# Depthwise convolution on TensorE: four 64x64 tiles that skip the empty blocks, output halves exchanged in every second batch, and running maxima in place of accumulators

## Chip, core and metric

The kernel runs on one core of one Trainium2 chip. The metric is the time of one execution in microseconds (us) on that core; the median of three timed runs stands for the kernel. The profile was taken from one more execution. Engines are named as in the profile: PE (TensorE matmul), PEld (TensorE weight load), DVE (VectorE), ACT (ScalarE), POOL (GpSimd), SP (SyncE, which issues the DMAs).

## What is computed

Two blocks in a row on 16 images of 32 channels and 32x32 pixels. The first is a dense block of dilated convolutions, a transform and a 3x3 convolution; the change does not touch it. The second is quantised, and the change is in its middle convolution, the depthwise one:

```python
def _fake_quant(x, bits):
    qmax = 2.0 ** (bits - 1) - 1.0
    scale = jnp.maximum(jnp.max(jnp.abs(x)) / qmax, 1e-08)
    y = x / scale
    yq = jnp.clip(y + jax.lax.stop_gradient(jnp.round(y) - y), -qmax - 1.0, qmax)
    return yq * scale
...
# x (16, 32, 32, 32), w1 (192, 32, 1, 1), w2 (192, 1, 3, 3), w3 (32, 192, 1, 1)
out = jax.nn.relu(_qconv(x, w1))
out = jax.nn.relu(_qconv(out, w2, stride=1, padding=1, groups=PLANES))
out = _qconv(out, w3)
return out + x
```

Each scale is the maximum over a whole tensor, so a convolution can start only when the whole output of the one before it is there and its maximum is known.

## The kernel before

`dense_block` runs first and takes about 346 us of the span. `quantised_block` then runs three stages, c1 (w1), c2 (w2, depthwise) and c3 (w3). The 192 planes are NG = 6 groups of 32, the 16 images are NB = 4 batches of BATCH = 4. The 128 partitions hold 32 channels for each of the four phases q of a pixel (its row and column modulo 2), so that a 3x3 convolution becomes, for each phase of the output, a sum over phases of the input with shifts of 0 or 1.

**c1.** PE multiplies the quantised input `xq` by the weights into PSUM (L1067), ACT (L905) and in every fourth tile DVE (L972) move the result through relu into `I` in SBUF, and DVE keeps a running maximum in `c1_most` (L981). Ahead of c1, DVE rounds the input: L957 and L962 for batches 0 and 1, L962 alone for batches 2 and 3, whose first step is ACT's (L900). At the same time POOL clears `c1_most` (L871), fills `minus_zero` (L872), which releases the semaphore `const`, and builds the first two diagonal weights (`build_diag`, L877).

**c2.** For each group g and batch b, DVE quantises `I` into `q2` (L997, two buffers by g % 2). PE then takes 4 taps t for each half h of the batch, 8 matmuls of 128x128 weights by 512 columns (L1084): partition block (input phase) to partition block (output phase), with a diagonal 32x32 block for each pair. ACT adds the bias, applies relu and writes `I` (L910). DVE reads it back, takes the maximum with an accumulator and writes it again (L1003, `peaks`). POOL builds `diag` for group g + 2 when c2 of group g is done (L877). The 8 PSUM banks hold 4 batches. PE's program for c2 is a loop over pairs of groups; DVE's order is `peaks(g)`, then `quantise(g + 2)`.

**Between c2 and c3.** DVE reduces the 24 maxima (L1016), PE transposes and spreads the result (L1047, L1051), DVE works out the scale (`rescale`), and PE puts the zero point's share into the banks (L1093).

**c3.** DVE and ACT quantise `I` in place (L1036, L916), PE sums over the 6 groups (L1108: 12 matmuls for a batch), DVE scales and adds the residual (L1030), SP stores it.

Order on each engine is the order of the code; engines meet through semaphores. Tile names are shown without numbers in the profile, so `q_c_most` there is `c1_most` (and, in the changed kernel, `c2_most` too).

## Time and profile before

| | us |
|---|---|
| median of 3 runs (lowest to highest) | 451.19 (450.24 to 451.94) |
| the profiled execution | 452.38 |
| its span, first to last instruction | 450.6 |
| PE, DVE, ACT, POOL busy | 395.0, 317.8, 213.6, 65.5 |
| c2, first to last matmul | 47.0 |

The span is what the trace covers; 1.8 us of the profiled execution lie around it. Busy times of the engines overlap each other, so they do not add up to the span: what sets the time in a stage is read from the chain of waits there.

### The profile page before, as it was taken

Reading aid. Unit: us, or ns where it says so; the run is one execution under the profiler, and the core shown is the slowest. Engines: PE = TensorE matmul, PEld = TensorE weight load, DVE = VectorE, ACT = ScalarE, POOL = GpSimd, SP = SyncE. Lnnn points to the kernel's source line nnn. Section 1 sums busy time; section 2 is a strip of 40 time slices with the busy share of each in tenths; the row PEclk is TensorE's granted clock in tenths of the full one; section 3 lists DMA queues with packets and bytes.
Section 4 is the critical chain, followed back from the end, with each engine's and each line's share of the span. In section 5 each row is a group of like instructions: output and inputs, shape, how many; then the busy total and the mean of one; then the engine's idle time right before and its main releaser. Section 6 shows DMA issues by size and latency. Waiting matters only on the chain. (4 is left out here: it accounts for less than half of the span.)

```text
span 450.6 us, 8168 instructions
## 1 busy us (share of the span) xinstructions
PE 395.0 (88%) x2890; PEld 273.3 (61%) x2892; DVE 317.8 (71%) x535; ACT 213.6 (47%) x346; POOL 65.5 (15%) x64
## 2 busy tenths in 40 slices
PE   1977999999999999999999999999494663999966
PEld 1755777687687768768776876877381221344422
DVE  7257666985697398569749857954916998598776
ACT  5135445453734545373454536426254882466550
POOL 6020320302112030211203022000302000001000
PEclk9998999999999999999999999999888697899989
DMA  7355225124432512443250342323000000000004
GB/s 242 87 156 156 66 65 141 52 71 101 127 81 51 156 35 69 102 127 81 61 150 26 75 104 64 83 70 94 1 1 0 1 1 0 0 0 0 0 3 186
DMA packets 19532, 32.54 MB, mean 72 GB/s; under 512 B 4528, under 2 KB 11568, under 8 KB 19504
## 3 DMA queue, kind: packets, MB, share of 16 engines
q1 hardware_dynamic: 19504, 32.17, 27.2%
q8 instruction: 17, 0.28, 0.3%
q14 instruction: 11, 0.09, 0.1%
HBM read 11.38 MB, written 2.10 MB: 30 GB/s over the span
## 5 line engine op out<-in xcount | busy, mean ns | idle before, releaser
L619 PE MATMUL sums_ps<-D,w_hl 128*128 128x512 f32 x576 | 149.5, 415 | 11.8 <-DVE w_hl L542 9.1
L619 PEld LDWEIGHTS sums_ps<-D,w_hl 128*128 128x128 f32 x576 | 109.3, 193 | 52.6 <-issue 14.9
L707 PE MATMUL mix_ps<-mix_hl,F_hl 128*128 128x288 f32 x360 | 66.5, 303 | 6.4 <-DVE St L445 6.0
L300 ACT ACTIVATE r<-sums_ps,bias_sb 64x512 f32<-64x512 f32 x32 | 21.9, 684 | 98.4 <-PE sums_ps L619 96.6
L335 ACT ACTIVATE Y<-mix_ps 128x288 f32<-128x288 f32 x120 | 49.0, 411 | 36.5 <-PE mix_ps L711 24.7
L707 PEld LDWEIGHTS mix_ps<-mix_hl,F_hl 128*128 128x128 f32 x360 | 57.3, 196 | 8.8 <-issue 6.8
L276 POOL CAST X<-X 32x512 fp32r<-32x512 f32 x32 | 27.7, 866 | 149.4 <-ACT X L326 147.8
L1084 PE MATMUL ps<-q_q,q_diag 128*128 128x512 bf16 x192 | 47.0, 408 | 1.5 <-DVE q_q L997 1.5
L401 DVE CAST D<-r 64x512 fp32r<-64x512 f32 x48 | 20.0, 416 | 32.8 <-ACT r L300 32.6
L403 DVE TENSOR_TENSOR D<-r,D 64x512 fp32r<-64x512 f32 x48 | 41.5, 864 | 1.6
L262 POOL TENSOR_TENSOR D<-x_own,D 128x576 fp32r<-128x576 f32 x16 | 25.4, 1607 | 113.9 <-ACT D L343 113.9
L910 ACT ACTIVATE q_I<-ps,w_bias 128x1024 f32 x24 | 26.8, 1115 | 28.3 <-PE ps L1084 28.3
L1084 PEld LDWEIGHTS ps<-q_q,q_diag 128*128 128x128 bf16 x192 | 19.1, 100 | 28.9 <-issue 3.6
L1003 DVE TENSOR_SCALAR_CACHE_REDUCE q_I<-q_I (+1 forms) x24 | 28.9, 1218 | 10.9 <-ACT q_I L910 10.8
L711 PE MATMUL mix_ps<-mix_hl,X 96*128 96x288 f32 x120 | 36.0, 305 | 0.0
L419 DVE SCALAR_TENSOR_TENSOR F_hl<-F,F_hl 128x1024 fp32r<-128x1024 f32 x16 | 19.6, 1224 | 23.1 <-ACT F_hl L317 22.8
L308 ACT ACTIVATE r<-sums_ps,bias_sb 64x512 f32<-64x512 f32 x32 | 22.0, 686 | 27.5 <-PE sums_ps L659 27.4
L428 DVE SCALAR_TENSOR_TENSOR X<-r,X 32x512 fp32r<-32x512 f32 x32 | 32.7, 1021 | 0.7
L659 PE MATMUL sums_ps<-D,w_hl 128*128 128x512 f32 x96 | 30.4, 427 | 2.6 <-DMA D<-D 2.6
L735 PE MATMUL mix_ps<-Y,hc 32*32 32x256 f32 x1080 | 28.8, 381 | 4.1 <-ACT Y L335 4.1
L438 DVE STREAM_TRANSPOSE Zt<-mix_ps 96x1024 f32<-96x1024 f32 x15 | 18.7, 1245 | 18.5 <-PE mix_ps L735 18.5
L735 PEld LDWEIGHTS mix_ps<-Y,hc 32*32 32x32 f32 x1080 | 19.0, 103 | 11.2 <-issue 8.4
(108 smaller groups left out, 445.7 us busy)
## 6 DMA issues: line engine op xcount, KB each, us to landing
D<-D SPq DMA_DIRECT2D x96, 126.0 KB, 2.4
F<-r SPq DMA_DIRECT2D x96, 64.0 KB, 2.0
x_own<-in_x_pads SPq DMA_DIRECT2D x16, 288.0 KB, 4.0
F<-in_x_mix SPq DMA_DIRECT2D x16, 128.0 KB, 2.5
xb<-in_x_res SPq DMA_DIRECT2D x8, 256.0 KB, 2.8
out<-q_res SPq DMA_DIRECT2D x8, 256.0 KB, 2.1
w_raw<-in_w_conv SPq DMA_DIRECT2D x6, 192.0 KB, 4.0
w_raw<-in_w_int SPq DMA_DIRECT2D x1, 843.0 KB, 4.6
```

Source lines behind the costliest of these rows:

```text
L276: nc.gpsimd.tensor_copy(X4[u][64:96, h], X4[u][32 * h:32 * h + 32, h].bitcast(F32)).then_inc(x4_copied[u], 1)
L335: nc.scalar.activation(Y[:, g], banks(p, u)[:, g % 4, 0:MIX], ACT.Copy).then_inc(y_out, 1)
L403: nc.vector.tensor_tensor(out=D[f][u][0:64, 1, :, 2:2 + S], in0=src, in1=D[f][u][0:64, 0, :, 2:2 + S].bitcast(F32), op=ALU.subtract).then_ ...
L428: last = nc.vector.scalar_tensor_tensor(out=X4[u][low, h], in0=r[u][k].rearrange("p a b l -> p (a b l)"), scalar=0.0, in1=X4[u][k, h].bitc ...
L619: last = nc.tensor.matmul(conv_ps[u][:, bank, :], w_hl[:, wp, n, d, :], D[f][u][:, xp, :, 2 * d:2 * d + S], start=start and d == 0 and h == 0,
L659: last = nc.tensor.matmul(bank, w_hl[:, 0, n, d, :], D[f - 1][u][:, 1, :, 2 * d:2 * d + S], start=False, stop=d == 2, skip_group_check=True)
L707: nc.tensor.matmul(y, F_hl[u][:, xp, h, k], mix_hl[:, wp], start=n == 0, stop=False, skip_group_check=True)
L711: nc.tensor.matmul(banks(p, u)[:, g % 4, 0:MIX], X4[u][:, g // 4, NP * (g % 4):NP * (g % 4) + NP], mix4_hl[:], start=False, stop=True, ski ...
L735: last = nc.tensor.matmul(out[32 * dy:32 * dy + 32, j, 0:PX // 4], hc[k, d], Y[k, :, at:at + 32], start=d == 0, stop=d == 2, skip_group_ch ...
L910: nc.scalar.activation(I[:, g, b, 0:PX], ps[:, 2 * b:2 * b + 2].rearrange("p k n -> p (k n)"), ACT.Relu, bias=keep.w2_bias[:, bass.ts(g, 1 ...
L1003: nc.vector.tensor_scalar(I[:, g, b, 0:PX], I[:, g, b, 0:PX], 0.0, 0.0, ALU.max, ALU.max, accum_out=c2_peak[:, g, b:b + 1]).then_inc(c2_pe ...
L1084: last = nc.tensor.matmul(ps[:, 2 * b + h], diag[:, par, 4 * t:4 * t + 4].rearrange("p q c -> p (q c)"), two[:, :, t // 2:t // 2 + PH, t % ...
```

## The change

In c2, two batches are now taken together, in 64x64 tiles. A tile (row, col) reads the partitions 64 * row and up and writes those at 64 * col and up; four such matmuls, one per tile, stand after each other in the code (`quarter`). Of the taps, those whose 64x64 block of weights is all zero are left out: where the input half equals the output phase half (`row == pi`), two taps stay of four. For this to give every tile the same amount of work, the halves of the output are exchanged in every second batch (`pi = col ^ b`). A pair of batches so takes 12 quarters, 48 matmuls of 64x64 by 512 columns, where it took 16 matmuls of 128x128 by 512 columns. Where a tile adds to a bank that the other row of tiles has begun, PE waits for `c2_half` (before quarters 4, 8 and 10). PE's program is written out without a loop; it waits for two batches of `q2` at a time and reports two at a time.

In c3 the odd batches use `w3_swap`, a copy of the weights with exchanged columns, which POOL makes once, behind the first two `build_diag`.

For groups 0 to 4 the maximum is kept in `c2_most` by an elementwise maximum, two tiles in turn; `fold_peaks` reduces it before the last group, whose maxima are taken as before (`last_peaks`). POOL clears `c2_most` (2048 elements a partition) ahead of `minus_zero`.

```diff
@@ -830,7 +830,9 @@
         Iq = I[:].bitcast(BF16)
         c1_peak = sb("c1_peak", [NP, NG // 2 * len(C1_DVE) + 1])
         c1_most = sb("c1_most", [NP, 2, 2, CUT], F16)
-        c2_peak = sb("c2_peak", [NP, NG, NB])
+        c2_peak = sb("c2_peak", [NP, NB + 1])
+        c2_most = sb("c2_most", [NP, 2, PX], F16)
+        w3_swap = sb("w3_swap", [NP, NG, NP], BF16)
         q2 = sb("q2", [NP, 2, NB, SLOT], BF16)
         diag = sb("diag", [NP, 2, 16, C], BF16)
         res = sb("res", [NP, 2, BATCH * PH * PH])
@@ -842,7 +844,8 @@
         stat_ready, turned, top_ready, spread = sem("stat_ready"), sem("turned"), sem("top_ready"), sem("spread")
         f_ready = sem("f_ready")
         x_rounded, x_rounded_dve, xq_ready = sem("x_rounded"), sem("x_rounded_dve"), sem("xq_ready")
-        c1_folded, c2_peaks = sem("c1_folded"), sem("c2_peaks")
+        c1_folded, c2_folded, c2_peaks = sem("c1_folded"), sem("c2_folded"), sem("c2_peaks")
+        c2_half, swapped = sem("c2_half"), sem("swapped")
         c1_done, c1_out, c1_out_dve = sem("c1_done"), sem("c1_out"), sem("c1_out_dve")
         q2_ready, diag_ready = sem("q2_ready"), sem("diag_ready")
         c2_done, c2_out = sem("c2_done"), sem("c2_out")
@@ -869,6 +872,7 @@
         def _(pool):
             nc.gpsimd.memset(zero_pt[:], ZERO)
             nc.gpsimd.memset(c1_most[:], 0.0)
+            nc.gpsimd.memset(c2_most[:], 0.0)
             nc.gpsimd.memset(minus_zero[:], -ZERO).then_inc(const, 1)
 
             def build_diag(g, par):
@@ -880,6 +884,10 @@
 
             build_diag(0, 0)
             build_diag(1, 1)
+            w3 = w_q[:, W1:W3].rearrange("p (g m) -> p g m", m=NP)
+            for half in (0, 64):
+                nc.gpsimd.tensor_copy(w3_swap[:, :, half:half + 64], w3[:, :, 64 - half:NP - half])\
+                    .then_inc(swapped, 1)
             with pool.Fori(0, NG // 2 - 1) as k:
                 for par in range(2):
                     pool.wait_ge(c2_done, k * (2 * NB) + (NB * par + NB))
@@ -920,6 +928,7 @@
         def _(dve):
             dve.sem_inc(c1_out_dve, GRANT)
             dve.sem_inc(c1_folded, GRANT)
+            dve.sem_inc(c2_folded, GRANT)
             done = [0]
 
             def link(ins):
@@ -1000,8 +1009,24 @@
             def peaks(g):
                 for b in range(NB):
                     dve.wait_ge(c2_out, g * NB + (b + 1 + GRANT))
+                    dve.wait_ge(c2_folded, g * NB + (b - 1 + GRANT))
+                    most = c2_most[:, b % 2]
+                    nc.vector.tensor_tensor(out=most, in0=most, in1=I[:, g, b, 0:PX],
+                                            op=ALU.max).then_inc(c2_folded, 1)
+
+            def fold_peaks():
+                dve.wait_ge(c2_folded, (NG - 1) * NB + GRANT)
+                link(nc.vector.tensor_tensor(out=c2_most[:, 0], in0=c2_most[:, 0], in1=c2_most[:, 1], op=ALU.max))
+                half = PX // 2
+                link(nc.vector.tensor_tensor(out=c2_most[:, 1, 0:half], in0=c2_most[:, 0, 0:half],
+                                             in1=c2_most[:, 0, half:PX], op=ALU.max))
+                nc.vector.tensor_reduce(c2_peak[:, NB:NB + 1], c2_most[:, 1, 0:half], AX.X, ALU.max)
+
+            def last_peaks(g):
+                for b in range(NB):
+                    dve.wait_ge(c2_out, g * NB + (b + 1 + GRANT))
                     nc.vector.tensor_scalar(I[:, g, b, 0:PX], I[:, g, b, 0:PX], 0.0, 0.0, ALU.max, ALU.max,
-                                            accum_out=c2_peak[:, g, b:b + 1]).then_inc(c2_peaks, 1)
+                                            accum_out=c2_peak[:, b:b + 1]).then_inc(c2_peaks, 1)
 
             quantise(0, 0)
             quantise(1, 1)
@@ -1011,9 +1036,10 @@
 
                     quantise(k * 2 + (par + 2), par)
             peaks(NG - 2)
-            peaks(NG - 1)
-            dve.wait_ge(c2_peaks, NT)
-            nc.vector.tensor_reduce(stat[:, 2:3], c2_peak[:], AX.XY, ALU.max).then_inc(stat_ready, 1)
+            fold_peaks()
+            last_peaks(NG - 1)
+            dve.wait_ge(c2_peaks, NB)
+            nc.vector.tensor_reduce(stat[:, 2:3], c2_peak[:], AX.X, ALU.max).then_inc(stat_ready, 1)
             rescale(2)
             nc.vector.tensor_tensor(out=last_scale[:], in0=sc[:, 2, 2:3], in1=keep.w_scale[:, 2:3],
                                     op=ALU.mult).then_inc(scale_read, 1)
@@ -1071,22 +1097,33 @@
             spread_stat(1)
             pe.wait_ge(c1_out_dve, NG // 2 * len(C1_DVE) + GRANT)
 
-            with pe.Fori(0, NG // 2) as k:
-                for par in range(2):
-                    pe.wait_ge(diag_ready, k * 2 + (par + 1))
-                    for b in range(NB):
-                        pe.wait_ge(q2_ready, k * (2 * NB) + (par * NB + b + 1))
-                        pe.wait_ge(c2_out, k * (2 * NB) + ((par - 1) * NB + b + 1 + GRANT))
-                        for h in range(2):
-                            two = q2[:, par, b, 2 * h * FIELD:2 * (h + 1) * FIELD]\
-                                .rearrange("p (m l i) -> p m l i", m=2, i=FS)
-                            for t in range(4):
-                                last = nc.tensor.matmul(
-                                    ps[:, 2 * b + h],
-                                    diag[:, par, 4 * t:4 * t + 4].rearrange("p q c -> p (q c)"),
-                                    two[:, :, t // 2:t // 2 + PH, t % 2:t % 2 + PH],
-                                    start=t == 0, stop=t == 3)
-                        last.then_inc(c2_done, 1)
+            def c2_pair(g, two):
+
+                par, sets = g % 2, (g * NB + two) // 2
+                pe.wait_ge(q2_ready, g * NB + two + 2)
+                if g:
+                    pe.wait_ge(c2_out, (g - 1) * NB + two + 2 + GRANT)
+                for n, quarter in enumerate(zip(*(c2_tile(row, col) for row in range(2) for col in range(2)))):
+                    if n in C2_TURNS:
+                        pe.wait_ge(c2_half, sets * 8 + C2_TURNS[n])
+                    for row, col, b, h, pi, u, v, first, final in quarter:
+                        rows = slice(64 * row, 64 * row + 64)
+                        field = q2[rows, par, two + b, 2 * h * FIELD:2 * (h + 1) * FIELD]\
+                            .rearrange("p (m l i) -> p m l i", m=2, i=FS)
+                        at = 4 * (2 * u + v) + 2 * pi
+                        last = nc.tensor.matmul(
+                            ps[64 * col:64 * col + 64, 2 * (two + b) + h],
+                            diag[rows, par, at:at + 2].rearrange("p q c -> p (q c)"),
+                            field[:, :, u:u + PH, v:v + PH], start=first and row == b,
+                            stop=final and row != b, skip_group_check=True)
+                        if final and row == b:
+                            last.then_inc(c2_half, 1)
+                last.then_inc(c2_done, 2)
+
+            for g in range(NG):
+                pe.wait_ge(diag_ready, g + 1)
+                for two in range(0, NB, 2):
+                    c2_pair(g, two)
 
             def zero_points(*banks):
                 for bank in banks:
@@ -1099,13 +1136,15 @@
             zero_points(3, 4, 5)
             pe.wait_ge(scale_read, 1)
             zero_points(6, 7)
+            pe.wait_ge(swapped, 2)
             for b in range(NB):
                 pe.wait_ge(q3_ready, b + 1)
                 pe.wait_ge(q3_act, b + 1)
                 for h in range(2):
                     bank = ps[:, 2 * b + h]
                     for g in range(NG):
-                        last = nc.tensor.matmul(bank, w_q[:, W1 + NP * g:W1 + NP * g + NP],
+                        w3 = w3_swap[:, g] if b % 2 else w_q[:, W1 + NP * g:W1 + NP * g + NP]
+                        last = nc.tensor.matmul(bank, w3,
                                                 Iq[:, g, b, HALF * h:HALF * h + HALF], start=False,
                                                 stop=g == NG - 1, skip_group_check=True)
                     last.then_inc(c3_done, 1)
@@ -1113,6 +1152,20 @@
 
 
 
+def c2_tile(row, col):
+
+
+
+
+
+    for b, h in ((0, 0), (0, 1), (1, 0), (1, 1)) if row == 0 else ((1, 0), (1, 1), (0, 0), (0, 1)):
+        pi = col ^ b
+        taps = [(u, v) for u in range(2) for v in ((row,) if row == pi else (0, 1))]
+        for n, (u, v) in enumerate(taps):
+            yield row, col, b, h, pi, u, v, n == 0, n == len(taps) - 1
+
+
+C2_TURNS = {4: 2, 8: 6, 10: 8}
 C1_TILES = 12
 C1_DVE = [2, 6, 10]
 C1_ACT = [j for j in range(C1_TILES) if j not in C1_DVE]
```

How the instructions stand on the engines, before and after the change. PE in c2, where its program for c2 begins (L1084 is the matmul of before, L1114 that of after):

Before:

```order
L1078 ISA [waits q_diag_ready]
L1084 MATMUL ps<-q_q,q_diag 128x512 [waits q_c2_out,q_q2_ready]
L1084 MATMUL ps<-q_q,q_diag 128x512 x7
L1078 REGISTER_ALU
L1084 MATMUL ps<-q_q,q_diag 128x512 [waits q_c2_out,q_q2_ready]
L1084 MATMUL ps<-q_q,q_diag 128x512 x7
L1078 REGISTER_ALU
```

After:

```order
L1114 MATMUL ps<-q_q,q_diag 64x512 [waits q_q2_ready,q_diag_ready,q_c1_out_dve]
L1114 MATMUL ps<-q_q,q_diag 64x512 x15
L1114 MATMUL ps<-q_q,q_diag 64x512 [waits q_c2_half]
L1114 MATMUL ps<-q_q,q_diag 64x512 x15
L1114 MATMUL ps<-q_q,q_diag 64x512 [waits q_c2_half]
L1114 MATMUL ps<-q_q,q_diag 64x512 x7
L1114 MATMUL ps<-q_q,q_diag 64x512 [waits q_c2_half]
L1114 MATMUL ps<-q_q,q_diag 64x512 x7
L1114 MATMUL ps<-q_q,q_diag 64x512 [waits q_q2_ready]
```

In place of eight matmuls behind each wait there are four stretches of 16, 16, 8 and 8 for a pair of batches, the last three behind `c2_half`, and no register instruction stands between them.

POOL at the start of `quantised_block` (`q_c1_most`, `q_c2_most` and `q_diag` are the tiles above):

Before:

```order
L870 MEMSET q_zero_pt 128x1
L871 MEMSET q_c_most 128x1544
L872 MEMSET q_minus_zero 128x512
L877 TENSOR_TENSOR q_diag<-blocks,w_q 128x512 x2
L883 UNCONDITIONAL_BRANCH
```

After:

```order
L873 MEMSET q_zero_pt 128x1
L874 MEMSET q_c_most 128x1544
L875 MEMSET q_c_most 128x2048
L876 MEMSET q_minus_zero 128x512
L881 TENSOR_TENSOR q_diag<-blocks,w_q 128x512 x2
L889 COPY q_w_swap<-w_q 128x6x64 x2
L891 UNCONDITIONAL_BRANCH
```

A second clearing stands ahead of `q_minus_zero`, whose end releases `const`, and two copies stand behind the two diagonals.

DVE at the end of c2, up to the reduction of the maxima. Before:

```order
L1008 REGISTER_ALU
L1008 COMPARE_AND_BRANCH
L1003 TENSOR_SCALAR q_I,q_c_peak<-q_I 128x1024 [waits q_c2_out] x8
L1016 TENSOR_REDUCE q_stat<-q_c_peak 128x1 [waits q_c2_peaks]
L939 TENSOR_TENSOR q_sc<-q_sc,w_scale 128x1
```

After:

```order
L1014 TENSOR_TENSOR q_c_most<-q_c_most,q_I 128x1024 [waits q_c2_folded,q_c2_out] x4
L1019 TENSOR_TENSOR q_c_most<-q_c_most 128x1024 [waits q_c2_folded]
L1021 TENSOR_TENSOR q_c_most<-q_c_most 128x512 [waits q_chain]
L1023 TENSOR_REDUCE q_c_peak<-q_c_most 128x1 [waits q_chain]
L1028 TENSOR_SCALAR q_I,q_c_peak<-q_I 128x1024 [waits q_c2_out] x4
L1042 TENSOR_REDUCE q_stat<-q_c_peak 128x1 [waits q_c2_peaks]
L948 TENSOR_TENSOR q_sc<-q_sc,w_scale 128x1
```

Three instructions that reduce `c2_most` stand between the maxima of group 4 and those of group 5; the four instructions of group 5 are what they were.

## Rows read from the trace of the kernel before

**Rows 1.** The page: busy us, share of the span, instructions; slices of PE in tenths.

```profile
PE 395.0 (88%) x2890; PEld 273.3 (61%) x2892; DVE 317.8 (71%) x535; ACT 213.6 (47%) x346; POOL 65.5 (15%) x64
...
PE   1977999999999999999999999999494663999966
```

**Rows 2.** The chain of waits in order of time: start us, us, what.

```profile
377.75 0.57 DVE q_c_peak L989
...
381.40 47.01 PE ps L1084 x192
...
428.54 1.12 ACT q_I L910
429.68 1.24 DVE q_I L1003 x2
430.94 0.19 DVE q_stat L1016
```

**Rows 3.** Line L1084 of c2: durations ns min/median/max, first and last start.

```profile
L1084 PEld LDWEIGHTS ps<-q_q,q_diag x192: 95/97/145, 381.4 to 427.8; 128*128 128x128 bf16 x192
L1084 PE MATMUL ps<-q_q,q_diag x192: 390/392/628, 381.4 to 428.0; 128*128 128x512 bf16 x192
```

**Rows 4.** C2 in order of time: start us, us, engine, what, idle before and its releaser.

```profile
380.83 3.54 DVE L997 TENSOR_SCALAR q_q<-q_I,q_sc 128x1158 bf16<-128x1158 f16 x8
...
382.24 0.14 PEld L1084 LDWEIGHTS ps<-q_q,q_diag 128*128 128x128 bf16 x1 [0.28 <-issue]
382.66 0.14 PEld L1084 LDWEIGHTS ps<-q_q,q_diag 128*128 128x128 bf16 x1 [0.28 <-issue]
...
403.28 1.21 DVE L1003 TENSOR_SCALAR_CACHE_REDUCE q_I<-q_I  x1
...
404.41 1.22 DVE L1003 TENSOR_SCALAR_CACHE_REDUCE q_I<-q_I  x1
```

**Rows 5.** Stretches of c2, all and L1084: length, busy (x touching), granted clock, DMA.

```profile
386.00:388.00 2.00, 2.00 (x8) 0.74 (x7) 1.23 (x2) 0.26 (x1) 0.00 (x0) 0.69 0.00 0
...
390.00:424.00 34.00, 34.00 (x149) 14.30 (x148) 1.00 0.00 0
```

**Rows 6.** Tiled matmuls of the transform, in order of time.

```profile
155.37 1.91 PE L735 MATMUL mix_ps<-Y,hc 32*32 32x256 f32 x72 [0.59 <-ACT Y L335]
...
160.33 1.91 PE L745 MATMUL mix_ps<-Zt,hr 96*32 96x256 f32 x16
```

**Rows 7.** Line L735: durations ns min/median/max.

```profile
L735 PE MATMUL mix_ps<-Y,hc x1080: 371/374/399, 64.8 to 334.5; 32*32 32x256 f32 x180
```

**Rows 8.** C1 in order of time, on ACT and on DVE, instructions that follow without a break.

```profile
364.62 6.47 ACT L905 ACTIVATE q_I<-ps 128x772 f32 x9 [0.54 <-PE ps L1067]
...
360.45 1.97 DVE L981 TENSOR_TENSOR q_c_most<-q_c_most,q_I 128x772 f16<-128x772 f16 x4
```

**Rows 9.** Line L1108 of c3 in a stretch: PE busy (x touching), PEld, granted clock, DMA.

```profile
439.00:444.40 5.40, 5.19 (x24) 1.95 (x22) 1.00 0.54 197
```

**Rows 10.** Start of the quantised block in order of time.

```profile
346.21 1.38 POOL L871 MEMSET q_c_most<- 128x1544 f16 x1
...
348.13 2.05 POOL L877 TENSOR_TENSOR q_diag<-blocks,w_q 128x512 bf16<-128x512 bf16 x2
...
349.30 1.50 DVE L957 TENSOR_SCALAR q_x_rnd<-fields,q_sc 128x1158 f32<-128x1158 f32 x1
...
351.51 0.82 DVE L957 TENSOR_SCALAR q_x_rnd<-fields,q_sc 128x1158 f32<-128x1158 f32 x1
```

**Rows 11.** POOL and DVE in the dense block, in order of time.

```profile
142.14 3.23 POOL L262 TENSOR_TENSOR D<-x_own,D 128x576 fp32r<-128x576 f32 x2 [15.89 <-ACT D L343]
142.18 1.92 DVE L403 TENSOR_TENSOR D<-r,D 64x512 fp32r<-64x512 f32 x1
```

**Rows 12.** Line L403: durations ns min/median/max.

```profile
L403 DVE TENSOR_TENSOR D<-r,D x48: 683/684/1924, 14.6 to 307.3; 64x512 fp32r<-64x512 f32 x48
```

**Rows 13.** The stretch after c2: length, busy PE, PEld, DVE, ACT, POOL, granted clock.

```profile
431.60:435.00 3.40, 3.40 (x9) 1.16 (x8) 1.92 (x8) 0.59 (x1) 0.00 (x0) 0.50 0.00 0
```

## The prediction

> **What bounds the kernel now.** I read the page's totals and slices first, then the chain of waits over the last 70 us, then c2 by stretches and in order of time. PE is busy for 88% of the span [rows 1], but the change touches only what comes after the dense block, from 346 us on. In the chain [rows 2], one piece stands out: PE's 192 matmuls of c2, 47.0 us from 381.40, without a break. Behind them come ACT's last batch, DVE's last maximum and the reduction at 430.94, 2.53 us after PE's end (428.41). So c2 is bound by PE, and each microsecond taken from its matmuls moves the end, until ACT or DVE become the bound.
>
> Two paces hold in c2. The granted clock is 0.5 (1.2 GHz) at first; its mean of 0.69 in the stretch from 386 to 388 [rows 5] puts the rise at about 387.2, 5.8 us after the first matmul. Until then matmuls follow each other by 0.427 us (the weight loads at 382.24 and 382.66 [rows 4]; the rows are rounded to 0.01). After it the clock is 1.0 (2.4 GHz) and 149 matmuls touch 34.0 us, the first and last in part [rows 5]: 0.230 us each. Check: 5.8 / 0.427 = 13.6 matmuls at the low clock, the other 178.4 at 0.230 make 41.0, and 0.2 for the end of the last: 47.0, as the chain has it.
>
> ACT and DVE have slack. A batch comes every 8 x 0.230 = 1.84 us; ACT needs 1.12 of it [rows 2]. DVE takes 1.13 for a maximum where two follow each other (403.28, 404.41) and (3.54 - 0.52) / 7 = 0.43 for a quantisation (eight in 3.54, the last one's own 0.52 taken off) [rows 4]: 1.56 of 1.84. DVE is the one that would bind next if it kept its work.
>
> **The change part by part.**
>
> *Matmuls.* A pair of batches takes 12 quarters in place of 16 full matmuls, so c2 takes 144 quarters in place of 192 matmuls. What a quarter costs is the question of this case: four 64x64 matmuls of 512 columns, each with its own weights. The trace of before has no bf16 tile of 64x64. The nearest rows are the transform's 32x32 tiles: 72 matmul records of 256 columns, 12 tiles, pass in 1.91 us [rows 6], though one lasts 0.374 [rows 7]. One after another at 0.230 / 512 = 0.45 ns a column they would take 8.3 us. They did run beside each other, six rounds of twelve in (1.91 - 0.37) / 6 = 0.26 us or less, with a weight load for each, in the same order of code (rows of tiles, then columns) that the change uses. So I take the pace of a quarter to be that of one full matmul with the same columns and the same strides, 0.230. The low end is 0.216, the pace of c3's matmuls, whose columns lie in one piece (24 in 5.19 us of busy time [rows 9]). The high end: a tile waits for its weights, 0.097 us a load [rows 3], so 0.327.
>
> From the first matmul on: 5.8 us at the low clock hold 13.6 quarters, the other 130.4 at 0.230 take 30.0, and 0.2 for the last: 36.0 in place of 47.0, **-11.0**. The first matmul now waits for two quantised batches, one more at 0.43: **+0.4**.
>
> *The waits on `c2_half`.* Quarter 4 may start when quarter 1 has ended. Quarter 1 ends 0.39 after its start, [rows 3]; quarter 4 is due 3 x 0.230 = 0.69 after that start. 0.3 us are left for the semaphore (0.1 from PE's end at 428.41 to ACT's start at 428.54 [rows 2]) and the weight loads (0.1). Quarter 10 waits for quarter 7 in the same way, quarter 8 has longer. The cover is thin: between 0 and 0.1 us each, 24 tight waits, 0 to 2.4 us; I take 0.03 each, **+0.7**. Only PE's own matmuls stand behind these waits.
>
> *ACT.* Its 24 instructions stay, but two become due at once. Back to back it does nine tiles of 772 elements in 6.47 us [rows 8]: (6.47 - 0.85) / 8 = 0.70 each, or 0.93 for 1024. Both banks' worth are out 0.1 + 0.93 + 1.11 = 2.1 us after a pair ends, and PE wants those banks 12 x 0.230 = 2.76 after it. Cost 0; if quarters fell to 0.18, ACT would set the pace.
>
> *DVE.* The elementwise maximum of 772 half-precision elements takes (1.97 - 0.56) / 3 = 0.47 [rows 8], so 0.62 for 1024. A pair costs 2 x (0.62 + 0.43) = 2.1 of 2.76 us: hidden. The quantised group g + 2 is there about 4 us after c2 of g ends, and is wanted after 5.5. With the old maxima it would have been 2 x 1.56 = 3.1 of 2.76, so this edit carries the other.
>
> *The end of c2.* ACT now does the last two batches after PE's last matmul, in place of one: batch 3 is out after 2.1 in place of 1.2. Ahead of the last maxima DVE folds `c2_most`: c1's reduction of 386 elements took 0.57 [rows 2], its maximum of 772 takes 0.56 with its own end [rows 8]; by length 0.70 (1024), some 0.44 (512) and 0.70 (the reduction of 512), 1.9 with their links. Group 4's last batch is out 3.4 before PE's end, folded at -0.7; then four maxima at 1.13 start at -0.7, 0.4, 1.6 and 2.7, and the last needs 1.26 (429.68 to 430.94). That is 3.95 after PE's end where 2.53 was: **+1.4**. If DVE were in time it would be +1.1.
>
> *The start of c1.* POOL now clears 2048 more elements (1.38 x 2048 / 1544 = 1.84 us) before `minus_zero`, and makes two copies behind the diagonals (by the two diagonals, 2.05 for 2 x 512 elements, some 0.7 each). `const` comes at about 350.4, DVE asks for it after 352: no wait. But POOL and DVE get in each other's way. The same rounding takes 1.50 beside POOL's diagonals and 0.82 after them [rows 10]. A DVE instruction whose median is 0.684 [rows 12] once took 1.92 [rows 11] and ended at 144.10, between the ends of two POOL instructions (142.14 to 145.37, so the first near 143.6): they take turns. The Trainium skill says so too (SBUF — State Buffer, "Who interferes with whom"): of a VectorE two-port instruction and a GpSimd one, the second to issue fully blocks. The trace agrees with it.
>
> In turns, DVE's six rounding instructions (0.6 to 0.7 each: 1.50 from 349.30 is 0.62 past the diagonals' end at 350.18) now meet clearing, `minus_zero`, two diagonals and two copies, where they met one diagonal. Counted through in turns, the first `xq` is there at about 351.3, where it was 351.6, and the last some 2.3 us later than before. c1's fifth tile, which needs all four, had 0.7 us of slack on it. ACT then runs nearly without a break [rows 8], so nothing gives this back: **+1.5**, between -0.5 (no meeting at all) and +3 (DVE gets no turn until POOL is through).
>
> *Free.* `w3_swap` is ready some 60 us early; c3 has the same matmuls. POOL's later diagonals take 1.03 [rows 10] against 4 us of slack. PE's code for c2 has no loop any more; parts of the dense block are written out as well, and PE's slices there stand at 9 [rows 1], so I price its fetching at 0.
>
> **Sum:** -11.0 + 0.4 + 0.7 + 1.4 + 1.5 = **-7.0 us**. The profiled execution took 452.38 (span 450.6), so the same one would take 445.4. It lies 1.2 above the median of the runs; 451.19 - 7.0 gives **444.2**.
>
> **The rivals.**
>
> *Weight loads show (slower).* If a tile cannot take new weights while its matmul runs, each quarter grows by up to a load, 0.097: 144 x 0.097 = +14, or +12.7 for the 130 at the high clock. The sum is then about +6: 457. It decides from 0.284 a quarter, since 7.0 / 130.4 = 0.054. For it: no row has 64-column loads, and the 96x32 tiles of rows 6 take 1.91 us for only 16 records, 0.4 for a round of four (their input is strided). Against it: the rounds of twelve.
>
> *PE drains at `c2_half`.* If each of the 36 waits lets the tiles run dry, each costs the end of a matmul (0.39 - 0.23 = 0.16) and a new start (0.1): 36 x 0.26 = 9.4 in place of 0.7, so 452.9. The burst of rows 6, which has both ends, costs 1.91 / 6 = 0.32 a round. Against it: the 0.3 us of cover.
>
> The Trainium skill has a rule that comes out there (TensorE: Matmul & The Clock Gate, "Measured speedup vs the span model"): four row tiles of 512 columns gained 3.07 times, not four. An estimate from that page: 4 x 0.230 / 3.07 = 0.30 a quarter, +9.1 on the sum. The trace does not bear it out where rounds follow each other; a single burst is nearer to it.
>
> *Half of the weight loads shows.* 0.28 a quarter: +6.5, so 450.7, not to be told from before.
>
> *DVE starves at the start of c1.* +1.5 more: 445.7.
>
> *The clock in c3.* Before, it was 0.5 from 431.6 to 435.0 [rows 13], and 1.0 in c3 [rows 9]. PE now idles 1.4 us longer there. If it comes back one such stretch later, the first batch of c3 takes 0.427 in place of 0.216 for 12 matmuls, +2.5, of which DVE hides little: 446.5.
>
> *Cheaper quarters.* At 0.216 and no stall, or no meeting with POOL: -2 to -3: 441.5.
>
> **How the numbers follow.** My forecast 0.53; c3's clock 0.12; DVE starved 0.10; cheaper 0.06; PE drains 0.07; weight loads in full 0.05; half of them 0.07. The last three, 0.19, are left out of the range: 440.5 (below the cheap case) to 449.5 (two of the dear ones together). About 0.5%, 2.3 us, is what a measurement can tell from no change. Below 448.9 lie the first four, 0.81, and a little of the half: faster 0.82. Between lie the rest of the half and a part of the drained case, 0.09; above, weight loads in full and the other part, 0.09.
>
> **What would show it.** c2 from first to last matmul near 36 us (0.327 a quarter gives 48.6, 0.216 gives 34); batches' ACT in pairs every 2.76; DVE idle in c2; PE's end to the reduction 3.6 to 4.0; the first ACT instruction of c1's steady run 1.5 later after the dense block. I am wrong if quarters cost over 0.25, if PE stops at quarters 4 and 10, or if the clock stays at 0.5 with tiles.

## The result, and the profile after

The changed kernel takes 444.6 us (median of 4 runs, 443.8 to 445.4), the kernel before on the same chip 450.7. The ratio on record is 0.985, with a 95% interval from 0.983 to 0.987 (the two medians alone give 0.986), so the kernel is faster by 1.3 to 1.7%. The forecast was 444.2, faster. Its profiled execution took 444.73 us, with a span of 442.9 where [rows 1] had 450.6: 7.7 less.

The page of the changed kernel: busy us of PE, and the slices of PE and of its granted clock in tenths, to be laid beside [rows 1].

```profile
PE 385.4 (87%) x3274; PEld 274.4 (62%) x3276; DVE 310.1 (70%) x518; ACT 212.6 (48%) x346; POOL 71.2 (16%) x67
...
PE   1978999999999999999999999999687285599686
...
PEclk9998999999999999999999999999969589599959
```

The line of c2's matmuls in the changed kernel (durations ns min/median/max), against [rows 3].

```profile
L1114 PEld LDWEIGHTS ps<-q_q,q_diag x576: 102/105/168, 382.0 to 416.6; 64*64 64x64 bf16 x192
L1114 PE MATMUL ps<-q_q,q_diag x576: 387/388/633, 382.1 to 416.8; 64*64 64x512 bf16 x192
```

There are three times as many matmuls and loads, each as long as one of before, so four matmuls must run at once. ACT's rows in c2 of the changed kernel in order of time (start us, us, engine, line, what, idle before and its releaser) give the pace of a pair of batches.

```profile
389.72 2.12 ACT L918 ACTIVATE q_I<-ps,w_bias 128x1024 f32 x2 [0.63 <-PE ps L1114]
...
398.02 2.12 ACT L918 ACTIVATE q_I<-ps,w_bias 128x1024 f32 x2 [0.66 <-PE ps L1114]
...
400.78 2.12 ACT L918 ACTIVATE q_I<-ps,w_bias 128x1024 f32 x2 [0.63 <-PE ps L1114]
```

Four pairs from 389.72 to 400.78 are 2.765 us a pair, 0.2304 for each of twelve quarters. ACT idles for 0.63 in each, so PE still sets the pace.

Stretches of the changed kernel: length, busy us of PE, PEld, DVE, ACT, POOL, granted clock, DMA. They answer to [rows 5, 13].

```profile
384.00:386.00 2.00, 2.00 (x24) 0.94 (x20) 0.51 (x2) 0.00 (x0) 0.00 (x0) 0.50 0.00 0
386.00:388.00 2.00, 2.00 (x40) 1.10 (x36) 0.00 (x0) 1.02 (x2) 0.00 (x0) 1.00 0.00 0
...
420.00:424.00 4.00, 2.30 (x7) 1.09 (x9) 1.93 (x7) 0.00 (x0) 0.00 (x0) 0.52 0.01 2
424.00:428.00 4.00, 3.26 (x9) 0.95 (x8) 3.86 (x7) 3.10 (x3) 0.00 (x0) 0.50 0.00 0
428.00:432.00 4.00, 4.00 (x15) 1.51 (x14) 1.75 (x4) 1.54 (x2) 0.00 (x0) 0.70 0.17 66
```

In c2 the clock rose at 386.0, 3.9 us after the first matmul (5.8 before). Behind c2 it fell to 0.5 and stayed there until about 430, well into c3. The forecast had left the time of that stage unchanged. The chain of waits of the changed kernel (start us, us, what) shows the end of c2 and the first batch of c3, against [rows 2]. The fence behind it has PE's rows of c3's first two batches in order of time.

```profile
412.84 1.12 ACT q_I L918
413.98 0.70 DVE q_c_most L1014
414.71 0.70 DVE q_c_most L1019
415.43 0.44 DVE q_c_most L1021
415.89 0.69 DVE q_c_peak L1023
416.58 4.57 DVE q_I L1028 x8
```

```profile
426.62 4.58 PE L1147 MATMUL ps<-q_I,w_q 128*128 128x512 bf16 x12 [0.74 <-DVE q_I L1062]
...
431.04 2.76 PE L1147 MATMUL ps<-q_I,q_w_swap 128*128 128x512 bf16 x12
```

The four last maxima on DVE now set the end of c2. The first batch's 12 matmuls take 4.58 us, the second's 2.76.

Last, the start of the quantised block in the changed kernel in order of time, against [rows 10].

```profile
346.40 1.81 POOL L875 MEMSET q_c_most<- 128x2048 f16 x1
...
347.90 0.92 DVE L966 TENSOR_SCALAR q_x_rnd<-fields,q_sc 128x1158 f32<-128x1158 f32 x1
...
348.14 1.14 POOL L876 MEMSET q_minus_zero<- 128x512 bf16 x1
...
349.36 2.95 POOL L881 TENSOR_TENSOR q_diag<-blocks,w_q 128x512 bf16<-128x512 bf16 x2
349.82 1.59 DVE L966 TENSOR_SCALAR q_x_rnd<-fields,q_sc 128x1158 f32<-128x1158 f32 x1
...
351.45 3.44 DVE L971 TENSOR_SCALAR q_xq<-q_x_rnd 128x1158 bf16<-128x1158 f32 x3
352.26 2.01 POOL L889 COPY q_w_swap<-w_q 128x384 bf16<-128x384 bf16 x2
```

Both engines are stretched: POOL's two diagonals take 2.95 where [rows 10] has 2.05, one rounding 1.59 where it is 0.82 without a neighbour.

The balance, from the two profiled executions (us). "Block" is DVE's reduction of the first statistic of the quantised block, from which c1 is counted:

| piece | before | after | difference | forecast |
|---|---|---|---|---|
| dense block, up to "block" | 346.5 | 345.5 | -1.0 | 0 |
| block to c2's scale (c1) | 34.23 | 35.42 | +1.2 | +1.5 |
| scale to c2's first matmul | 0.64 | 1.17 | +0.5 | +0.4 |
| c2, first to last matmul | 47.00 | 35.13 | -11.9 | -10.3 (-11.0, waits +0.7) |
| PE's end to the reduction | 2.54 | 3.97 | +1.4 | +1.4 |
| reduction to the last result | 17.14 | 19.27 | +2.1 | 0 |

Before rounding, the differences add up to -7.64, and the span shows -7.65. The first row is scatter: the same code of the dense block reached "block" between 344.5 and 348.2 in the thirteen profiles of this study.

### The profile page after: what moved, and what is told of

The parts are those of the page before. It is cut to its first block and busy times, and to the rows that moved or that the text cites. A ratio compares the mean times of both kernels' runs of the same rounds, so it can differ in the third digit from the quotient of the medians.

```text
span 442.9 us, 8893 instructions
## 1 busy us (share of the span) xinstructions
PE 385.4 (87%) x3274; PEld 274.4 (62%) x3276; DVE 310.1 (70%) x518; ACT 212.6 (48%) x346; POOL 71.2 (16%) x67
## 5 line engine op out<-in xcount | busy, mean ns | idle before, releaser
L403 DVE TENSOR_TENSOR D<-r,D 64x512 fp32r<-64x512 f32 x48 | 41.5, 865 | 1.6
L1114 PE MATMUL ps<-q_q,q_diag 64*64 64x512 bf16 x576 | 35.1, 403 | 2.0 <-DVE q_q L1006 2.0
L918 ACT ACTIVATE q_I<-ps,w_bias 128x1024 f32 x24 | 25.4, 1111 | 19.2 <-PE ps L1114 19.2
L735 PE MATMUL mix_ps<-Y,hc 32*32 32x256 f32 x1080 | 28.8, 381 | 4.1 <-ACT Y L335 4.1
L1114 PEld LDWEIGHTS ps<-q_q,q_diag 64*64 64x64 bf16 x576 | 19.8, 109 | 16.9 <-issue 3.6
L735 PEld LDWEIGHTS mix_ps<-Y,hc 32*32 32x32 f32 x1080 | 19.0, 103 | 11.2 <-issue 8.4
L1093 PE MATMUL ps<-q_xq,w_q 128*128 128x386 bf16 x72 | 17.4, 381 | 9.1 <-DVE q_xq L971 5.2
```

The lines of the kernel that those rows point to most:

```text
L403: nc.vector.tensor_tensor(out=D[f][u][0:64, 1, :, 2:2 + S], in0=src, in1=D[f][u][0:64, 0, :, 2:2 + S].bitcast(F32), op=ALU.subtract).then_ ...
L735: last = nc.tensor.matmul(out[32 * dy:32 * dy + 32, j, 0:PX // 4], hc[k, d], Y[k, :, at:at + 32], start=d == 0, stop=d == 2, skip_group_ch ...
L1093: last = nc.tensor.matmul(c1_slot(ps, j)[:, h], w_q[:, bass.ts(k * 2 + par, NP)], xq[:].rearrange("p b n -> p (b n)")[:, at:at + CUT], sta ...
L1114: last = nc.tensor.matmul(ps[64 * col:64 * col + 64, 2 * (two + b) + h], diag[rows, par, at:at + 2].rearrange("p q c -> p (q c)"), field[: ...
```

## The experiments

"c1", "c2", "end of c2" and "c3" are the pieces of that table. All kernels are made from the changed one. Those that add matmuls for PE overwrite their results; none leaves a part of the computation out.

### Is c2's gain the skipped blocks, and what do the maxima carry?

**All taps.** The tiles and their order stay, but the empty blocks are computed too, 16 quarters a pair.

```diff
-        taps = [(u, v) for u in range(2) for v in ((row,) if row == pi else (0, 1))]
+        taps = [(u, v) for u in range(2) for v in (0, 1)]
-C2_TURNS = {4: 2, 8: 6, 10: 8}
+C2_TURNS = {8: 4, 12: 8}
```

> The changed kernel with no tap left out: each tile does four taps for every half, the empty 64x64 blocks too, so 16 quarters for a pair of batches in place of 12; c2_half is waited for before quarters 8 and 12. Theory (a quarter costs what one full matmul costs, tiles by themselves give nothing): c2 grows by 48 quarters x 0.230 = 11 us, to about 46, and the time to 455.6, above the kernel before by the 5 us that c1's start, the end of c2 and c3's clock cost. Rival (tiles are cheaper in themselves): below 453.

Measured: 456.27 us, 1.0068 of before (1.0032 to 1.0103); c2 took 47.07. ACT in c2 of this kernel in order of time:

```profile
397.01 2.12 ACT L918 ACTIVATE q_I<-ps,w_bias 128x1024 f32 x2 [1.57 <-PE ps L1114]
...
400.69 2.12 ACT L918 ACTIVATE q_I<-ps,w_bias 128x1024 f32 x2 [1.56 <-PE ps L1114]
```

A pair comes every 3.68 us, 16 x 0.230. Four 64x64 matmuls cost what one 128x128 costs, and without the skipping the tiles gain nothing: c2 is as long as before (47.00), and the rest of the change (c1 +1.2, first matmul +0.5, end +1.2, c3 +2.4) makes the kernel slower. The whole gain is the quarter of the work that is left out.

**Tiles with the old maxima.** DVE goes back to the maximum with accumulator, and the fold is gone.

```diff
-                    nc.vector.tensor_tensor(out=most, in0=most, in1=I[:, g, b, 0:PX],
-                                            op=ALU.max).then_inc(c2_folded, 1)
+                    nc.vector.tensor_scalar(I[:, g, b, 0:PX], I[:, g, b, 0:PX], 0.0, 0.0, ALU.max, ALU.max,
+                                            accum_out=c2_peak[:, bass.ts(g * NB + b, 1)])\
+                        .then_inc(c2_peaks, 1)
...
-            fold_peaks()
-            last_peaks(NG - 1)
+            peaks(NG - 1)
```

> The changed kernel with the maxima of before: all 24 by the instruction with an accumulator that also writes its input back, no c2_most kept and none folded (POOL still clears it). Theory (tiles need the cheap maxima): DVE needs 2 x (1.13 + 0.43) = 3.1 us for a pair, PE 2.77, so DVE sets the pace in the middle of c2; c2 gets 3 to 4 us longer, less 0.3 at its end: 447.5 to 448.5. Rival (PE sets the pace anyway): 444.3.

Measured: 448.64 us, 0.9942 (0.9918 to 0.9966); c2 took 38.97. DVE in c2 of this kernel, in order of time:

```profile
400.32 2.61 DVE L1006 TENSOR_SCALAR q_q<-q_I,q_sc 128x1158 bf16 x4
402.85 1.21 DVE L1012 TENSOR_SCALAR_CACHE_REDUCE q_I<-q_I  x1
...
407.41 2.55 DVE L1006 TENSOR_SCALAR q_q<-q_I,q_sc 128x1158 bf16 x4
```

DVE never idles here: a group takes 407.41 - 400.32 = 7.1 us, where PE needs 2 x 2.765 = 5.5. So DVE becomes the bound. It also costs clock. c2 began with 3.4 us at 0.5, a little less than the changed kernel's 3.9. Between 407 and 411 PE then waited for `q2` and was busy for only 1.9 of 4 us, and from 410.3 to 413.7 the granted clock was at 0.5 once more, in the middle of c2. That second stretch can be worth at most 1.7 of the 3.8 us that c2 is longer; how the 3.8 divide between DVE's pace and the clock isn't shown, but both come from DVE.

**The maxima with the old matmuls.** PE's loop of before, everything else of the change.

```diff
-            for g in range(NG):
-                pe.wait_ge(diag_ready, g + 1)
-                for two in range(0, NB, 2):
-                    c2_pair(g, two)
+            with pe.Fori(0, NG // 2) as k:
...
+                            for t in range(4):
+                                last = nc.tensor.matmul(
+                                    ps[:, 2 * b + h],
+                                    diag[:, par, 4 * t:4 * t + 4].rearrange("p q c -> p (q c)"),
```

> The changed kernel with the 128x128 matmuls of before (the loop too) and the old weights in c3; running maxima, folding and POOL's clearing and copies stay. Theory (the matmuls carry the whole gain): c2 47 us as before, c1 1.2 us longer, so about 452, not under 450.7. Rival (the maxima are part of the gain by themselves): under 450.

Measured: 453.54 us, 1.0036 (1.0005 to 1.0066). In its chain of waits c2 is one piece again:

```profile
382.93 46.55 PE ps L1110 x192
```

c2 is bound by PE, as before; the running maxima gain nothing there, and POOL's added work costs its 1.2 us at c1. Neither half of the change brings the whole gain alone: the ratios are 0.994 and 1.004, together 0.985.

### How do the tiles share PE's queue?

The forecast rested on matmuls of different tiles standing next to each other in the code. If the overlap needs that, two matmuls of a tile in a row must break it.

```diff
-                for n, quarter in enumerate(zip(*(c2_tile(row, col) for row in range(2) for col in range(2)))):
+                four = [list(c2_tile(row, col)) for row in range(2) for col in range(2)]
+                for n in range(0, 12, 2):
+                    quarter = [t[m] for t in four for m in (n, n + 1)]
```

> The changed kernel with the same 48 matmuls for a pair in another order: each tile gets two of its matmuls in a row before the next tile's turn. Theory (PE starts matmuls strictly in order, so only neighbours in different tiles overlap): two quarters take four times 0.23 in place of twice, c2 doubles from 35 to about 68 us, and the time is near 476. Rival (each tile takes its own from the queue): 444.6, as the changed kernel.

Measured: 445.31 us, 0.9818 (0.976 to 0.9875); c2 36.02. ACT in c2 of this kernel in order of time:

```profile
395.43 2.12 ACT L918 ACTIVATE q_I<-ps,w_bias 128x1024 f32 x2 [0.65 <-PE ps L1116]
398.18 2.12 ACT L918 ACTIVATE q_I<-ps,w_bias 128x1024 f32 x2 [0.63 <-PE ps L1116]
...
400.96 2.12 ACT L918 ACTIVATE q_I<-ps,w_bias 128x1024 f32 x2 [0.65 <-PE ps L1116]
```

(400.96 - 395.43) / 2 = 2.765, the same pace to three figures. My theory fell and the rival held: the order of the code can't be the order of the starts, or the pace would be twice as long. A tile's next matmul must be passed by the other tiles' ones. c2 is 0.9 longer only because 5.9 us of it, not 3.9, ran at the low clock. How far does that go? Four in a row (`range(0, 12, 4)`, and the waits on `c2_half` set to `{4: 6, 8: 8}`):

> The changed kernel with four matmuls of a tile in a row before the next tile's turn; to keep the banks apart, c2_half is then waited for before the 5th and 9th of each tile, for all that stands before. Two in a row had left the pace at 2.77 us a pair. Theory (each tile takes its own matmuls from a queue that holds them all): 16 matmuls still take 4 x 0.23, and two full waits for the tiles to run dry add about 0.3 us each, so 3.4 us a pair, c2 43 us, the time about 452. Rival (only near neighbours overlap): 16 matmuls take nearer to 2 us or more, a pair 6 us and up, c2 over 70 us, the time over 480.

Measured, one run: 453.18 us. PE in c2 of this kernel in order of time:

```profile
390.97 3.37 PE L1116 MATMUL ps<-q_q,q_diag 64*64 64x512 bf16 x48 [0.20 <-PE ps L1116]
...
394.54 3.37 PE L1116 MATMUL ps<-q_q,q_diag 64*64 64x512 bf16 x48 [0.20 <-PE ps L1116]
```

3.57 us a pair, and 44.4 us for c2: dearer than 2.765, but far from 48 x 0.230 = 11 one after another, and near the theory's 3.4. The same view shows where the 0.80 goes. First one stretch of 16 matmuls between two waits, then the weight loads of PE; each of these rows begins as a wait ends.

```profile
408.83 1.15 PE L1116 MATMUL ps<-q_q,q_diag 64*64 64x512 bf16 x16 [0.20 <-PE ps L1116]
```

```profile
394.54 0.64 PEld L1116 LDWEIGHTS ps<-q_q,q_diag 64*64 64x64 bf16 x16 [0.71 <-PE ps L1116]
...
395.83 1.58 PEld L1116 LDWEIGHTS ps<-q_q,q_diag 64*64 64x64 bf16 x32 [0.65 <-PE ps L1116]
...
398.11 0.64 PEld L1116 LDWEIGHTS ps<-q_q,q_diag 64*64 64x64 bf16 x16 [0.71 <-PE ps L1116]
```

The 16 matmuls between two waits take 1.15: three steps of 0.23 and the last one's own 0.39 make 1.08, so four matmuls of a tile in a row still run at the pace of the changed kernel. From one wait to the next, 394.54 to 395.83, are 1.29 us for four rounds (0.92); the next eight rounds take 2.28 (1.84). So the two waits of a pair cost 0.37 and 0.44, together the whole 0.80: at each the tiles run dry, and PE has no matmul for 0.14 to 0.20 of it. No limit to what can wait at a tile shows up to four.

### What the start of c1 costs

POOL's clearing of `c2_most` goes behind c1's last matmul, and the two copies behind the later diagonals.

```diff
-            nc.gpsimd.memset(c2_most[:], 0.0)
...
+            pool.wait_ge(c1_done, NG // 2 * C1_TILES)
+            nc.gpsimd.memset(c2_most[:], 0.0).then_inc(c2_zeroed, 1)
...
+            dve.wait_ge(c2_zeroed, 1)
```

> The changed kernel with POOL's new work moved: c2_most is cleared once c1's matmuls are done, and w3_swap is copied behind the last diagonal. Nothing else differs. Theory (POOL and DVE block each other at the start of c1): the stretch from the start of the quantised block to the end of c1 was 1.2 us longer than before and loses that again, so about 443.4 where the changed kernel has 444.6; the fifth tile of c1 starts some 1.5 us sooner. Rival (the clock, or nothing in particular, made c1 longer): c1 as long as in the changed kernel, 444.6.

Measured: 444.99 us, 0.985 (0.9817 to 0.9884). The start of the quantised block of this kernel, in order of time:

```profile
349.68 2.04 POOL L880 TENSOR_TENSOR q_diag<-blocks,w_q 128x512 bf16<-128x512 bf16 x2
...
350.84 1.50 DVE L967 TENSOR_SCALAR q_x_rnd<-fields,q_sc 128x1158 f32<-128x1158 f32 x1
...
353.05 0.82 DVE L967 TENSOR_SCALAR q_x_rnd<-fields,q_sc 128x1158 f32<-128x1158 f32 x1
...
353.90 2.11 DVE L972 TENSOR_SCALAR q_xq<-q_x_rnd 128x1158 bf16<-128x1158 f32 x3
```

These are the durations of [rows 10] again; three roundings take 2.11, not 3.44. c1's fifth tile starts 8.53 us after "block" (before 8.63, changed 9.55), and c1 is 34.45 long: 0.97 of the 1.19 are back. So POOL's added work was the main cause. It wasn't the only one, because c1 also begins at the low clock: the clock rose 10.0 us after "block" in the kernel before, 13.2 in the changed one and 11.7 in this one. In the profile of the next kernel, with POOL's work where the change has it (fifth tile at 9.55 again) but the clock back at 10.3, c1 took 34.82; in the eight others with POOL's work there and the clock back at 11.75 to 13.6 it took 35.42 or 35.43. So POOL's work costs 0.6 us where the clock comes back early and 1.0 where it comes back late; the rest of the 1.2 is the clock's. The median doesn't show that microsecond: it is less than the scatter of the runs, and in the profile the dense block ended 2.7 us later.

### What the clock in c3 costs

PE gets 18 matmuls behind c2, so that it is not idle while ACT and DVE finish.

```diff
+            pe.wait_ge(c2_out, NT - 2 + GRANT)
+            for n in range(18):
+                nc.tensor.matmul(ps[:, 0], keep.w3_sum[:], minus_zero[:], start=True, stop=True,
+                                 skip_group_check=True)
```

> The changed kernel with 18 extra matmuls of 128x128 by 512 columns into PSUM bank 0, which is free there, between c2 and the transpose of the maxima, where PE otherwise idles 4.3 us. Their result is overwritten. Theory (the late rise of the clock costs c3's first batch 2.1 us): the granted clock stays at 1.0, the 12 matmuls of the first batch take 2.8 in place of 4.6 us, and the time is about 442.5. Rival (c3's first batch is late for its input, or the reduction of the maxima is what costs): 444.6, or 445 and more if the extra matmuls stand in the way of the transpose.

Measured: 443.32 us, 0.9822 (0.9771 to 0.9873). PE behind c2 of this kernel in order of time (the record of one of the 18 is missing):

```profile
418.75 3.83 PE L1136 MATMUL ps<-q_minus_zero,w_sum 128*128 128x512 bf16 x17 [0.16 <-issue]
...
427.06 2.75 PE L1151 MATMUL ps<-q_I,w_q 128*128 128x512 bf16 x12 [1.35 <-DVE q_I L1062]
```

The first batch takes 2.75 in place of 4.58, and the small matmuls of the scale are quicker too: c3 is 16.50 long, not 19.27. The 2.77 us are shown in the profile. The intervals of the two ratios overlap, but the granted clock of every run agrees: its mean over the span was 0.958 to 0.969 in the four runs here and 0.950 to 0.954 in the ten runs of the changed kernel. Was the slow first batch chance? The changed kernel, run again:

> The changed kernel as it is, beside e11 on the same chip, to see how its time spreads: by its first runs a ratio of 0.985 to the kernel before, 0.983 to 0.987. Theory (c3's first batch at the low clock is the usual case): the profile again has 12 matmuls in 4.3 to 4.9 us there. Rival (it was one draw): 2.8 us.

Measured: 444.38 us, 0.985 (0.9817 to 0.9882). The stretch and PE's row of the first batch in this run:

```profile
424.00:428.00 4.00, 3.26 (x8) 0.90 (x7) 3.14 (x2) 4.00 (x4) 0.00 (x0) 0.50 0.00 0
```

```profile
425.52 4.45 PE L1147 MATMUL ps<-q_I,w_q 128*128 128x512 bf16 x12 [0.74 <-DVE q_I L1062]
```

It is the usual case, though not the only one, as the next kernel shows.

### Can the end of c2 be shorter?

The fold moves ahead of group 4, whose maxima then use the accumulator like group 5's.

```diff
-                dve.wait_ge(c2_folded, (NG - 1) * NB + GRANT)
+                dve.wait_ge(c2_folded, (NG - 2) * NB + GRANT)
...
-            peaks(NG - 2)
             fold_peaks()
+            last_peaks(NG - 2)
             last_peaks(NG - 1)
```

> The changed kernel with the running maxima folded after group 3; groups 4 and 5 both take their maxima with the accumulator. Theory (DVE is late for the last maxima by the folding): from PE's last matmul to the reduction 3.6 in place of 3.97 us, the time about 444.2. Rival (ACT's last batch sets it): 3.97 as it is.

Measured, one run: 443.12 us, the end of c2 4.71 long. DVE there, in order of time:

```profile
412.16 1.21 DVE L1028 TENSOR_SCALAR_CACHE_REDUCE q_I<-q_I 128x1024 f16<-128x1024 f16 x1
...
420.13 1.22 DVE L1028 TENSOR_SCALAR_CACHE_REDUCE q_I<-q_I 128x1024 f16<-128x1024 f16 x1
...
421.39 0.16 DVE L1042 TENSOR_REDUCE q_stat<-q_c_peak 128x1 f32<-128x9 f32 x1
```

The theory fell. Eight maxima at 1.14 now stand in a row, 9.1 us from the end of the fold, and DVE has no slack to hide them in; the changed order, with four, is the better. The run was quick all the same because in it the clock was at 1.0 in c3 (first batch 2.75, c3 17.44) and c2 had 2.9 us at the low clock: an example of how one run misleads.

### Together

First all of it (POOL late, the early fold, 16 matmuls between c1 and c2, 18 ahead of c3):

> The changed kernel with POOL's new work moved as in e1, extra matmuls before c3 as in e2, 16 more of them between c1 and the spreading of its maxima, and the folding after group 3. Theory: -1.2 at the start of c1, -2.1 in c3, -0.3 at the end of c2, and about -2 in c2, whose first 3.9 us ran at the low clock: 444.6 - 5.6 = 439. Rival (the clock falls anyway in the gaps that are left before c2, or the extra matmuls delay what follows): 441 or more.

Measured: 441.93 us, 0.9748 (0.9691 to 0.9806): the rival held. Two stretches of this kernel:

```profile
382.00:386.00 4.00, 3.84 (x40) 2.24 (x44) 2.60 (x7) 0.00 (x0) 0.00 (x0) 0.57 0.00 0
...
428.00:432.00 4.00, 4.00 (x15) 1.61 (x14) 1.89 (x4) 1.42 (x2) 0.00 (x0) 0.74 0.19 70
```

The clock fell in both places although PE had been given work: between that work and c2, and in c3, PE still idled for the scale. c3's first batch took 4.44, with the same 18 matmuls ahead of it that had been enough in the profile above. The end of c2 was 4.91, the early fold's. The last kernel drops the fold, and puts work also into those gaps: 9 matmuls ahead of c1, 16 and 7 around the scale of c2, 18 and 3 around that of c3.

```diff
+            busy(9, w_q[:, 0:HALF])
...
+            busy(16, minus_zero[:])
             spread_stat(1)
+            busy(7, minus_zero[:])
...
+            pe.wait_ge(c2_out, NT - 2 + GRANT)
+            busy(18, minus_zero[:])
...
+            busy(3, minus_zero[:], 6)
```

> The changed kernel with POOL's new work moved as in e1 and PE kept busy in its gaps by matmuls whose results are overwritten: 9 ahead of c1, 16 and 7 around the spreading of c1's maxima, 18 ahead of the transpose of c2's, 3 before the last zero points; the folding stays where the change has it. Theory (what is left of the cost is POOL against DVE at the start of c1, and the clock in c2 and c3): c1 1.0 us shorter, c2 33.5 in place of 35.1, c3 2.8 shorter: 444.6 - 5.4, about 439. Rival (the clock falls all the same, or the matmuls stand in the way): 442 or more.

Measured: **437.66 us** (436.85 to 441.84, 6 runs), 0.9708 of before (0.9667 to 0.9748), on the chip where the changed kernel had 0.985 (0.9817 to 0.9882). Two stretches of this kernel, the first just behind the start of c2 (379.35) and the second around that of c3 (421.18):

```profile
380.00:384.00 4.00, 4.00 (x77) 2.28 (x72) 1.96 (x6) 1.53 (x2) 0.00 (x0) 1.00 0.02 4
...
420.00:424.00 4.00, 3.29 (x17) 1.31 (x15) 3.48 (x4) 4.00 (x4) 0.00 (x0) 1.00 0.00 0
```

c1 is 32.89 long, c2 33.35 (144 x 0.2304 and the last one's own end), c3 16.50: against the profile of the changed kernel -2.5, -1.8 and -2.8, together 7.1, and the profiled executions differ by 444.73 - 437.49 = 7.2. c1 gained 1.5 us more than the forecast had for it: the clock was back 5.5 us after "block", and 1.0 of the 2.5 is POOL's moved work.

## Why the prediction was right, step by step

**The matmuls, -11.0 and +0.7; measured -11.9.** The pace of 0.230 a quarter, the question of the case, was right to the third figure. The row that it leaned on carries less than the prediction made of it. Six rounds of twelve have five steps between them, so [rows 6] give (1.91 - 0.37) / 5 = 0.31 us a round, not 0.26, while 256 columns at 0.45 ns each are 0.115. They show that tiles run beside each other, not that a round costs what one matmul costs; that was a guess until the kernel with all taps showed it (47.07 against 47.00). Two sizes were off. The waits on `c2_half` cost nothing: a pair takes 12 x 0.2304 with three waits in it, so 0.3 us of cover is enough (-0.7). And the low clock lasted 3.9 us, not the 5.8 carried over from before (-0.9); in the other profiles of kernels with tiles, the last one aside, it lasted between 2.9 and 5.9 at the start of c2. Half of that difference is time, so the term scatters by 1.5 us from run to run, which the forecast did not allow for.

**The dear rivals.** Neither weight loads nor draining showed: loads of 0.105 stay hidden under running matmuls, also of the same rows of the array. Where the tiles do run dry, in the kernel with four in a row, a wait costs 0.4, more than the 0.26 of that rival. The Trainium skill says otherwise of loads and order in TensorE: Matmul & The Clock Gate, "What overlaps and what doesn't": weight loads overlap only where the row group differs, and matmuls start and end strictly in order. Here four tiles without a pause have a matmul running on each row group at each load, and the pace is 4.0 matmuls in the time of one; two in a row of one tile keep it, where strict order would have made some 476 us of the kernel. The measurement decides. Nor do these four tiles, in a stream, gain the 3.07 times of four row tiles that the prediction took from the Trainium skill (same page, "Measured speedup vs the span model"): they gain 4.0. No run has a single burst of four, so what one would gain is not shown.

**The start of c2, +0.4; measured +0.5.** As forecast.

**DVE and ACT hidden in c2.** Both held; the tiles with the old maxima show that one edit carries the other. The forecast of 3.1 us a pair for the old maxima was low, since a quantisation of four takes 2.6 beside POOL's diagonal; measured 3.5.

**The end of c2, +1.4; measured +1.4** (3.97, forecast 3.95), by the chain that was named: fold, then four maxima in a row.

**The start of c1, +1.5; measured +1.2.** The first tile came earlier (4.69 after "block", before 5.35) and the fifth later (9.55, before 8.63), as counted in turns. That is 0.9; the other 0.3 is the clock, which rose later and which the forecast for c1 left out.

**c3, 0; measured +2.1. This step failed.** The rival with 0.12, priced at +2.5, is what happened in 7 of the 9 profiles of kernels with the change or a part of it and no work added ahead of c3. The prediction put the term at 0 and gave no reason but that before the clock had come back by 435.0. What the runs show in its place: the clock came back at 430.4, 3.7 us into c3, and the 12 matmuls of the first batch took 4.58 in place of 2.76. Work for PE ahead of c3 took it away in two of the three profiles that had such work (2.75, and 4.44 with all put together). Whether the clock comes back in time isn't settled by the length of the gap alone. From c2's last matmul to c3's first are 7.7 and 8.0 us in the two kernels with the old matmuls, where the batch was quick; 8.2 to 9.4 in the seven profiles where it was slow; but 10.2 in the kernel with the early fold, where it was quick again. What else decides it stays open.

So the total is right partly by luck: +2.1 in c3 stands against -0.7 of waits that were free, -0.9 of a shorter low clock, -0.3 at c1 and -1.0 of scatter in the dense block. With c3's cost added to the forecast it would have been 446.3; the range held both.

## What to carry to other kernels

Zero blocks of 64x64 can be left out at full value: count the blocks, give each of the four tiles the same number (no run here tried unequal ones), and price a round of four as one full matmul. A gain of PE shows in full only if the engine behind it keeps up, here because it was relieved in the same step. Every gap that the change opens in PE's work is to be priced with the clock of the stage behind it; where it falls, matmuls with no use in the gap can be worth nearly as much as the change itself (here 0.985 to 0.971, of which about 1 us was POOL's moved work). A piece of POOL's work that is needed later does not belong beside DVE's work on the path.

## What the runs showed of the hardware

- The four tiles take their matmuls independently of the order of the code: one or two in a row of a tile give 2.765 us for 48. Four in a row give 3.57, all of the difference at the two waits; 16 matmuls between waits still take four steps of 0.23.
- A wait of PE on its own matmuls of three rounds back costs nothing (three of them in 12 x 0.2304); a wait on those just issued costs 0.4.
- The granted clock after a gap is not the same from run to run: with tiles and no work in the gaps c2 began with 2.9 to 5.9 us at 0.5 (1.2 GHz), and c3's first batch took 2.75 or 4.4 to 5.1. With work in all gaps it was 1.0 (2.4 GHz) in all of c2 and c3, and came back 6 to 8 us sooner in c1. By the profiles this is worth about 6 us of this kernel.
- Beside DVE's rounding, POOL takes 1.03 us for a copy of 384 half-precision elements a partition (0.7 was estimated); the first of the two moved copies took 0.50. A clearing of 512 stretches from 0.52 to 1.14.
